# A gated cross-attention block: V products ahead of the value products, small products moved to their bank, the context transposed in a later step

## What is computed

```python
def xattn(x, context):                  # x is layernormed before, and again inside
    q = (layernorm(x, gamma, beta) @ w_q)        # 16 heads of 64
    k, v = split(context @ w_kv)
    attn = softmax(einsum('bqhd,bkhd->bhqk', q * SCALE, k))
    out = einsum('bhqk,bkhd->bqhd', attn, v) @ w_out + b_out
    return out * tanh(gate)
x = x + tanh(g_xattn) * xattn(layernorm(x), ctx)
x = x + tanh(g_ffn) * ffn(layernorm(x))
```

## Time and profile before

| | |
|---|---|
| median of three runs | 475.88 us (473.37 to 476.15) |
| span of the profiled execution | 473.7 us; the page gives no other time for it |
| PE busy | 439.7 us, 93% of the span |
| ACT busy | 386.4 us, 82% |
| DVE busy | 360.3 us, 76% |
| POOL busy | 356.6 us, 75% |
| instructions | 13155 |

### The profile page before, as it was taken

The page is one execution under the profiler, slowest core; times in us unless marked ns, Lnnn a source line. Parts: engine busy times, 40 slices in busy tenths (PEclk is TensorE's granted clock), DMA queues, the critical chain, the costliest instruction groups (busy, mean ns, idle before and its releaser), DMA issues.

```text
span 473.7 us, 13155 instructions
## 1 busy us (share of the span) xinstructions
PE 439.7 (93%) x5096; PEld 334.0 (71%) x5096; DVE 360.3 (76%) x789; ACT 386.4 (82%) x630; POOL 356.6 (75%) x270
## 2 busy tenths in 40 slices
PE   7889799998999989999999999999999999988993
PEld 6656667776767767776777667776777677758892
DVE  4787687778877887779787796878877887785622
ACT  5889788899888988899888898899799998892330
POOL 3687686888788887888878877898878877871325
PEclk9999999999999999999999999999999999999998
DMA  5499999999999999999999999999989998996021
GB/s 167 150 177 192 206 187 175 170 181 204 188 176 188 210 194 180 192 192 192 198 189 197 189 196 191 185 200 209 190 157 185 193 180 147 159 182 137 14 67 46
DMA packets 283037, 82.10 MB, mean 173 GB/s; under 512 B 264387, under 2 KB 280435, under 8 KB 282976
## 3 DMA queue, kind: packets, MB, share of 16 engines
q1 hardware_dynamic: 281600, 77.96, 93.4%
q0 software_dynamic: 1376, 3.30, 2.2%
HBM read 10.83 MB, written 5.14 MB: 34 GB/s over the span
## 4 chain that ended last, share of the span: by engine, by line
PE 40%; DVE 20%; ACT 16%; DMA 10%; issue 8%; POOL 4%; POOLq 0%; SPq 0%; ACTq 0%; DVEq 0%
DVE MXL L903 9%; DMA PT<-PARTS 9%; ACT P L752 7%; DVE HL L890 4%; ACT HL L714 4%; PE psAB L1234 3%; PE psX L1319 3%; PE psAB L1241 3%; PE psO L1267 3%; ACT PARTS L762 3%; POOL PARTS L650 3%; PE psX L1355 3%; DVE VL L896 3%; PE psO L1269 3%; PE psO L1268 3%
## 5 line engine op out<-in xcount | busy, mean ns | idle before, releaser
L650 POOL TENSOR_TENSOR PARTS<-P,PARTS 128x1024 f16<-128x1024 f32 x125 | 267.4, 2145 | 63.5 <-ACT PARTS L762 61.8
L762 ACT ACTIVATE PARTS<-P 128x1024 f16<-128x1024 f32 x126 | 136.1, 1080 | 0.7
L752 ACT ACTIVATE P<-psAB,NB 128x512 f32<-128x512 f32 x128 | 81.6, 695 | 41.8 <-DVE NB L906 41.4
L903 DVE TENSOR_REDUCE MXL<-psAB 128x2 f32<-128x1024 f32 x64 | 78.4, 1224 | 41.4 <-PE psAB L1241 23.9
L1267 PE MATMUL psO<-VH,PT 128*128 128x65 f16 x1008 | 98.6, 194 | 8.3 <-DMA PT<-PARTS 7.7
L1267 PEld LDWEIGHTS psO<-VH,PT 128*128 128x128 f16 x1008 | 92.0, 98 | 12.0 <-DMA PT<-PARTS 8.9
L1268 PE MATMUL psO<-VL,PT 128*128 128x64 f16 x1008 | 98.5, 192 | 0.0
L1269 PE MATMUL psO<-VH,PT 128*128 128x65 f16 x1008 | 98.4, 193 | 0.0
L1268 PEld LDWEIGHTS psO<-VL,PT 128*128 128x128 f16 x1008 | 91.3, 98 | 0.5
L1269 PEld LDWEIGHTS psO<-VH,PT 128*128 128x128 f16 x1008 | 91.5, 97 | 0.0
L752 ACT ACTIVATE P<-psCD,NB 128x512 f32<-128x512 f32 x128 | 81.7, 703 | 0.1
(11 more groups left out here) (214 smaller groups left out, 871.7 us busy)
## 6 DMA issues: line engine op xcount, KB each, us to landing
ctx_raw<-in_ctx_dram SPq DMA_DIRECT2D x8, 256.0 KB, 3.7
w1s<-in_L_ffn_w_dram SPq DMA_DIRECT2D x8, 256.0 KB, 3.6
w2s<-in_L_ffn_w_dram SPq DMA_DIRECT2D x8, 256.0 KB, 4.0
PT<-PARTS SPq DMA_TRANSPOSE x126, 5.0
experts_table<-zeros POOLq DMA_DIRECT2D x2, 645.0 KB, 4.0
X<-in_x_dram SPq DMA_DIRECT2D x8, 128.0 KB, 4.2
wraw<-in_L_xattn_w_kv_dram SPq DMA_DIRECT2D x4, 256.0 KB, 5.3
out_dram<-row SPq DMA_DIRECT2D x8, 128.0 KB, 2.5
```

Of the source, the lines that this page charges most:

```text
L650: pool.tensor_tensor(PARTS[:, par, qt, 1], P32[:, par, qt], PARTS[:, par, qt, 0], ALU.subtract).then_inc(plo_done, 1)
L752: last = act.activation(P32[:, par, qt, SK * h:SK * h + SK], score_bank(qt)[:, SK * h:SK * h + SK], ACT.Exp, bias=NB[:, par, qt, h:h + 1])
L762: act.activation(PARTS[:, hp % 2, qt, 0], P32[:, hp % 2, qt], ACT.Copy).then_inc(phi_done[qt], 1)
L903: dve.tensor_reduce(MXL[:, par, qt, :, 0], score_bank(qt)[:].rearrange("p (h n) -> p h n", h=2), AX.X, ALU.max, negate=True).then_inc(max_ ...
```

## The change

Four things are moved; no arithmetic is added or removed.

- The small products of all batches but the last write psO instead of psX. A second memory, `wait_o`, makes the next writer of psO wait for the last reader, and the value products go through it as well. psX keeps the V products and the context transposes (and the small products of the last batch behind the loop).
- On PE the small products and the context transposes stand right behind the scores, ahead of K and Q of the next pair. The V product of every step stands ahead of the value products.
- The context of the next batch is transposed in step 5 (`CTX_STEP` is 4 instead of 2, and the transposes stand one step behind it); ACT's and DVE's parts of it follow, and SP loads the next context in step 6 instead of 3.
- The readers: the copies of the transposed queries and tokens go from ACT to DVE, ahead of its second row maximum, as do the first reads of the expert choice and of the ranks. ACT's high part of V goes ahead of the second `phi`. `add_part` and `add_attention` stay where they were on DVE, behind `kq_lo`.

```diff
-        PART_STEP, CTX_STEP, PROJECT_STEP = 1, 2, 3
+        PART_STEP, CTX_STEP, PROJECT_STEP = 1, 4, 3
...
         def x_bank(b):
-            return psX[:, 0:SQ] if b else psO
+            return psO[:, 0:SQ]
...
# SP
-                    if hp == CTX_STEP + 1 and b + 2 < B:
+                    if hp == CTX_STEP + 2 and b + 2 < B:
                         sp.wait_ge(ctxt_psum, b + 2)
                         sp.dma_start(ctx_raw[:], ctx_t[b + 2]).then_inc(ctx_in, 16)
...
# ACT, batch
-                    if hp == X_STEP and not is_last(b):
-                        xt_copy(b + 1)
-                    if hp == TOKT_STEP and not is_first(b):
-                        tokt_copy(b - 1)
                     if j < LAST:
                         phi(b, hp, 0)
                     exps(b, hp, 1)
                     if ot_pair(j) >= 0:
                         ot_copy(ot_pair(j))
+                    if hp != CTX_STEP and v_group(b, hp):
+                        v_hi(*v_group(b, hp))
                     if j < LAST:
                         phi(b, hp, 1)
-                    if hp != CTX_STEP and v_group(b, hp):
-                        v_hi(*v_group(b, hp))
...
# DVE, new
+            def xt_copy(b):
+                dve.wait_ge(xt_psum, b + 1)
+                dve.wait_ge(norm_scaled, 1)
+                dve.wait_ge(xt_lo_done, b)
+                dve.tensor_scalar(XS[:], x_bank(b), norm_q[:, 0:1], norm_q[:, 1:2], ALU.mult, ALU.add)\
+                   .then_inc(xt_f32, 1)
+            def tokt_copy(b):
+                dve.wait_ge(tokt_psum, b + 1)
+                dve.tensor_copy(tT[:], psO[:, 0:QT * P]).then_inc(tokt_done, 1)
...
-            def add_part(b, part, bank=psX):
+            def add_part(b, part, bank=psO):
...
+            def take_ranks(b):
+                ranks = ps_ranks(b).rearrange("p (t e) -> p t e", e=E)
+                dve.wait_ge(pos_psum, b + 1)
+                dve.tensor_tensor(rank_hot[:], ranks[:, 0:QT, :], hot, ALU.mult).then_inc(route, 1)
+                dve.tensor_copy(taken[:], ranks[:, QT, :]).then_inc(route, 1)
...
# DVE, batch
-                    row_max(b, hp, 1)
+                    if hp == RANKS_STEP and b > 1:
+                        take_ranks(b - 2)
+                    if hp == X_STEP and not is_last(b):
+                        xt_copy(b + 1)
+                    if hp == TOKT_STEP and not is_first(b):
+                        tokt_copy(b - 1)
...
-                    if hp == LOGITS_STEP and not is_first(b) and not is_last(b):
+                    if hp == LOGITS_STEP and not is_first(b):
                         choose(b - 1)
+                    if j == LAST:
+                        take_ranks(B - 2)
+                    row_max(b, hp, 1)
+                    if hp == LOGITS_STEP and not is_first(b):
+                        first_winner(b - 1)
...
# PE
+            o_free = [None]
+            def wait_o(free_when):
+                if o_free[0]:
+                    pe.wait_ge(*o_free[0])
+                o_free[0] = free_when
...
             # values
-                if j:
-                    pe.wait_ge(norm_done, turn(j) - 1)
-                else:
+                wait_o((norm_done, turn(j)))
+                if j == 0:
                     pe.wait_ge(row_consts, 1)
...
-            def project_part(b, pairs, bank=psX):
-                if bank is psX:
+            def project_part(b, pairs, bank=psO):
+                if bank is psO:
+                    wait_o((part_done, b + 1))
+                elif bank is psX:
                     wait_x((part_done, b + 1))
...
             def project(b):
-                wait_x((x1_done, b + 1))
+                wait_o((x1_done, b + 1))
...
# PE, batch
                     scores(b, hp, 1)
+                    if hp == CTX_STEP + 1 and not is_last(b):
+                        ctx_transposes(b + 1)
+                    # ranks, project_part, project, x_transposes,
+                    # tok_transposes, router_weights, logits: here, as below
                     if ahead:
                         k_project(*next_pair(b, hp, AHEAD))
                         q_project(*next_pair(b, hp, AHEAD))
                     if ot_pair(j) >= 0:
                         o_transposes(ot_pair(j))
-                    # the same seven, and the V product of CTX_STEP among them
+                    if v_group(b, hp):
+                        v_project(*v_group(b, hp))
                     if VALUES_BEHIND <= j < LAST:
                         values(*back(b, hp, VALUES_BEHIND))
-                    if hp == CTX_STEP and not is_last(b):
-                        ctx_transposes(b + 1)
-                    if hp != CTX_STEP and v_group(b, hp):
-                        v_project(*v_group(b, hp))
```

More of the change, by code:

```diff
@@ L191, in gated_block, with ps_logits, ps_ranks @@
         psX = pb("psX", [P, 512])
-        ps_logits = psX[:, 0:QT * E]
-        ps_ranks = psX[:, 0:(QT + 1) * E]
-        ps_gw_mid = psX[:, 0:E]
+        def ps_logits(b):
+            return (psX if b == B - 1 else psO)[:, 0:QT * E]
+        def ps_ranks(b):
+            return (psX if b == B - 1 else psO)[:, 0:(QT + 1) * E]
+        ps_gw_mid = psO[:, 0:E]
         x_in = sem("x_in")
@@ L1018, in place @@
                 dve.tensor_copy(taken[:], ranks[:, QT, :]).then_inc(route, 1)
+            def place(b):
+                n = b * ROUTE
                 dve.wait_ge(lexp_done, b + 1)
@@ L1101, in _ @@
             normalise_heads(B - 1, PAIRS - 3)
-            add_part(B - 1, B - 1)
+            add_part(B - 1, B - 1, psX)
             normalise_heads(B - 1, PAIRS - 1)
@@ L1279, in o_transposes, with tok_transposes @@
                 last.then_inc(ot_psum, pairs)
-            def tok_transposes(b, bank=psX):
-                if bank is psX:
-                    wait_x((tokt_done, b + 1))
+            def tok_transposes(b, bank=psO):
+                if bank is psO:
+                    wait_o((tokt_done, b + 1))
                 pe.wait_ge(x1_done, B - 1 + QT if is_last(b) else b + 1)
@@ L1289, in logits @@
             def logits(b):
-                wait_x((route, b * ROUTE + 4))
+                (wait_x if b == B - 1 else wait_o)((route, b * ROUTE + 4))
                 pe.wait_ge(tokt_done, b + 1)
@@ L1293, in logits @@
                 for q in range(QT):
-                    last = pe.matmul(ps_logits[:, E * q:E * q + E], tT[:, P * q:P * q + P], gw_mid[:], start=True, stop=True)
+                    last = pe.matmul(ps_logits(b)[:, E * q:E * q + E], tT[:, P * q:P * q + P], gw_mid[:], start=True, stop=True)
                 last.then_inc(logit_psum, 1)
             def router_weights():
-                wait_x((gw_mid_done, 1))
+                wait_o((gw_mid_done, 1))
                 pe.wait_ge(gw_in, 16)
@@ L1332, in ranks @@
                 carried = taken[:].unsqueeze(1).to_broadcast([P, QT + 1, E])
-                pe.matmul(ps_ranks.rearrange("p (t e) -> p t e", e=E), ident[:], carried, start=True, stop=False)
+                pe.matmul(ps_ranks(b).rearrange("p (t e) -> p t e", e=E), ident[:], carried, start=True, stop=False)
                 for i, (counts, c) in enumerate(((tri, 2), (ones_bf, 1), (ones_bf, 0))):
-                    last = pe.matmul(ps_ranks, counts[:], hot_padded[:, c:c + QT + 1, :].rearrange("p t e -> p (t e)"),
+                    last = pe.matmul(ps_ranks(b), counts[:], hot_padded[:, c:c + QT + 1, :].rearrange("p t e -> p (t e)"),
                                      start=False, stop=(i == 2))
@@ L1349, in project @@
             def project(b):
-                wait_x((x1_done, b + 1))
+                wait_o((x1_done, b + 1))
                 pe.wait_ge(ot_done, b * PAIRS + PAIRS)
                 for qt in range(QT):
-                    dst = psX[:, D * qt:D * qt + D]
+                    dst = psO[:, D * qt:D * qt + D]
                     for pair in range(PAIRS // 2, PAIRS):
@@ L1386, in _ @@
             v_project(0, 0, 1, psO)
+            o_free[0] = (v_lo_done, 2)
             def batch(b):
@@ L1394, in batch @@
                     scores(b, hp, 1)
+                    if hp == CTX_STEP + 1 and not is_last(b):
+                        ctx_transposes(b + 1)
+                    if hp == RANKS_STEP and b > 1:
+                        ranks(b - 2)
+                    if j == LAST:
+                        ranks(b - 1)
+                    if hp == PART_STEP and not is_first(b):
+                        project_part(b - 1, range(PAIRS // 2))
+                    if hp == PROJECT_STEP and not is_first(b):
+                        project(b - 1)
+                    if hp == X_STEP and not is_last(b):
+                        x_transposes(b + 1)
+                    if hp == TOKT_STEP and not is_first(b):
+                        tok_transposes(b - 1)
+                    if hp == LOGITS_STEP and is_first(b):
+                        router_weights()
+                    if hp == LOGITS_STEP and not is_first(b):
+                        logits(b - 1)
```

39 lines of the change are left out of this document (9 added, 30 removed).

## The result

The changed kernel took 489.11 us (488.15 to 492.26, four runs), the kernel before on the same chip 475.98 (473.37 to 476.15). The ratio is 1.0317, 95% interval 1.0269 to 1.0364: 3.2% slower. The forecast was 498.4 with a range of 486 to 506. The profiled span grew from 473.7 to 486.9 us, so by 13.2 where the sum had 22.5.

The account below looks back on a forecast made before the run. The prediction took the tensor engine, 93% busy, as the bound. Its terms, 24.9 - 4.4 - 4.3 + 2.1 + 3.4 + 0.8 = 22.5 us, took the span from 473.7 to 496.2; with 2.2 more, 498.4 us, range 486 to 506.

Parts of the forecast that it names:

- the sum: Whole kernel: all predicted losses and gains together lengthen the profiled span of 473.7 us by 22.5 us.
- The holds: Steps 1 and 3, batches 1 to 7: value products wait for VectorE's additions, 14 times 1.78, 24.9 us.
- The context transposes: End of step 2: their wait behind the V product in psX goes, 0.73 in six batches, 4.4 us back.
- Waits of the scores: Second scores wait about 0.3 more in step 3 and 0.49 in step 5; 2.1 and 3.4 us in seven batches.
- Relief of the waits for PT: Value products wait less for transposed exponentials, four of six waits in steps 6 and 7: 4.3 us, ends 2.0 and 7.7.
- The last step: Its second row maximum starts later, behind the counts of ranks and two small reads: 0.8 us lost.
- what was open in the kernel before: Tensor engine, steady batch: matmuls fill 50.48 of 51.56 us, so little more than a microsecond is open to better order.
- The rule that was weighed: Tensor engine: by weight-load busy time, 14.15 us a batch are free; the prediction sided instead with closed-up matmul groups.
- the holds vanish in slack: Rival, steps 1 and 3: tensor engine slack absorbs the holds, only gains remain, 467.2 us; chance 0.05.
- no hold came in part only: Rival: split or addition comes sooner than batch 7 shows, say half of each hold, 486 us; chance 0.12.
- the transposes did not come late: Rival: context load pushes step 6's transposes by 1.15 in six batches, value products' waits not relieved, 509.6 us; chance 0.09.
- V ahead does nothing for these waits: Rival: the later fp16 copy eats the relief of the waits for transposed exponentials, 502.7 us; chance 0.1.

Follow-up runs that it names:

- experiment 1: Changed kernel with the two additions that read the half projections moved ahead of VectorE's split of the next K and Q; 471.5 us, ratio 0.9899.
- experiment 2: Changed kernel with the two half projections back behind the output transposes, still writing psO; 470.49 us, ratio 0.9886.
- experiment 5: Changed kernel with `CTX_STEP` set back from 4 to 2, so the next context is transposed in step 3; 490.52 us, ratio 1.0304.
- experiment 6: On top of experiment 1, token moments moved behind step 4's second row maximum, POOL's part a step later; 469.9 us, ratio 0.9914.
- experiment 4: On top of experiment 3, eight filler products into psX ahead of the value products in steps 1 and 3; 503.81 us, ratio 1.0611.
- experiment 3: Changed kernel with V product behind value products and ScalarE's V copy behind the second fp16 copy again, except step 4; 518.29 us, ratio 1.0861.

## Why the prediction was right, and which step of it was off

The sign, the place and the mechanism were right, and the time lay inside the range, 9.3 below the forecast (489.11 against 498.4). That the time fell inside the range is in part luck: the lower end was set for holds of half the length, and they came whole; the room was taken by gains that the sum had left out. By its own steps:

- **The holds.** Said: 14 times 1.78 in steps 1 and 3, 24.9 us. Measured: the time from the V product's start to the value products is 2.59 in steps 1 and 3 and 0.81 in the others, so 1.78 more, 14 times. Experiments 1 and 2 take the holds away, by moving the reader and by moving the writer, and the loss goes with them. They were priced from the kernel before, by the chain in batch 7, though nothing waited for that chain there.
- **The context transposes.** Said 0.73 a batch. From the start of the value products of step 2 to the next group it was 2.28 and is 1.55. Right; experiment 5 shows that the step number has no part in it.
- **Waits of the scores.** Said 0.3 in step 3 and 0.49 in step 5. Measured 0.34 (0.80 to 1.14) and 0.44 (1.20 to 1.64) in batches 1 to 6. For step 5 it had named the V copy and the moments; without that copy in step 4 (experiment 5) the wait is 0.50 shorter, with the moments later (experiment 6 against 1) 0.27, so both have a part. In batch 7 step 3 the second scores had waited more before (1.63, now 1.15), which the sum did not see.
- **Relief of the waits for PT.** Said 4.3 between 2.0 and 7.7, measured 6.8 (7.7 to 0.9): 2.5 better, inside its ends, but not where it was placed. The prediction looked for it in steps 6 and 7, behind grown steps; 4.1 of the 6.8 came in batch 0, which has no holds (4.3 to 0.2). For batches 1 to 7 (3.4 to 0.7) the runs do not agree: without the holds the waits there are 6.3 in experiment 1 and 1.0 in experiment 2. How much of the relief is due to V ahead, to the holds or to chance is open.
- **The last step.** Said 0.8. From the first scores of the last step to the end of the span the kernel took 0.6 more.
- **The step that failed: what was open in the kernel before.** The prediction ("What bounds the kernel now", "What the change takes away") counted only waits that the tensor engine's matmul rows show, and concluded that little more than a microsecond per batch was open. The weight loads of the small products had waits of their own for VectorE's split of V, and once a batch for that of the context, in the kernel before:

```profile
PEld psX L1294 <- DVE VL L896: 2.4, 7, 1.3
...
PEld psX L1319 <- DVE VL L896: 2.0, 7, 0.3
PEld psX L1365 <- DVE VL L896: 1.8, 7, 0.3
PEld psX L1286 <- DVE VL L896: 1.6, 7, 0.2
...
PEld psX L1355 <- DVE cT_lo L877: 1.1, 6, 0.2
```

These are 8.9 us of idle weight loads. But for 1.1 us (line 1294, once) no matmul row shows idle time there, since the rows ahead are drawn to overlap it. The starts show it: in steps 1 and 3 to 6 of the kernel before, the next group follows the output transposes by 0.33 to 0.42, where without a wait it follows by 0.16 to 0.22, depending on which group it is. Against 0.22 that is some 0.8 a batch. For the two projections experiment 2, which holds their place fixed, shows that it goes with the bank psX (0.20 and 0.11). For the other small products, which were moved in the order as well, it is argued from the same wait.

The account of the 9.3 us that the sum was too high on the span: 2.5 from PT. From the output transposes to the next group, and in the small products, the eight steps took 1.02 less per batch net, in batches 1 to 6 6.1, and 0.1 in batch 7; in that stands a new wait of 0.58 in step 4 (the V product there now waits for the split of V, seen above), without which it would be 1.6. The score waits of batch 7 came out 1.0 lower than the sum had them. In step 0 the scores took 0.14 more per batch, which gives back some 0.9. That makes 8.8 of 9.3; the rest is not placed. Part of the 1.02 is no wait but the account itself: a group's time to the next start depends on which group follows it. And the 2.5 from PT is little more than the 2 us by which these waits differ in batch 0 alone between two executions of the same instructions.

**The rule that was weighed.** The prediction set the closed sequence of matmul groups against the Trainium skill, Perfetto Trace Analysis, section Identifying the Most-Contended Engine, by which matmul busy time says little of how near TensorE is to its limit. For the holds the trace sided with the sequence: 1.78 came out as 1.78. For the gains it sided with the Trainium skill. The same 5096 matmuls were busy 439.7 us before and 435.1 after, in a kernel that waits more: what looked like a full engine held 8.9 us in which weight loads waited for a bank. The rival that the holds vanish in slack did not come about; the slack was there, elsewhere in the step.

The other rivals: no hold came in part only, and the transposes did not come late (0.9 us of waits for PT). That V ahead does nothing for these waits is not refuted: in experiment 4, where V stands behind the value products and the holds are there, they are 1.6.

## What to carry to other kernels

When a small product moves to another bank, look at where its reader stands on the reader's own engine. The bank's next writer then waits for everything queued ahead of that reader, here a split that itself depends on products issued later; the length of that chain can be read from the kernel before, even where nobody waits for it. To see how much a busy tensor engine has left, list the waits of its weight loads as well and compare start-to-start times of one group across steps, with the same group behind it: the differences show waits that overlapping matmul rows hide. And before a difference in waits between two profiles is put down to a change, look at a stretch that the change does not touch.

## What the runs showed of the hardware

In experiment 3 the lower granted clock came at 11 of 14 idle stretches of 2.35 us and slowed what stood behind it (values in up to 2.6 us instead of 1.45). In the changed kernel it came at none of the 14 holds with 1.65 us of idle time; the rows behind the holds keep 1.00:

```profile
288.00:291.00 3.00, 1.35 (x14) 1.00 1.31 163
291.00:300.00 9.00, 8.83 (x128) 1.00 1.05 212
```

The length of the idle stretch alone does not decide it. In the same execution of the changed kernel, in batch 0, the clock fell once behind an idle stretch of 1.60:

```profile
26.10 0.96 PE L1274 MATMUL psCD<-HL 64*128 64x512 f32 x6 [1.60 <-ACT P L753]
```

```profile
27.50:30.90 3.40, 3.40 (x26) 0.50 1.13 213
```

The 0.7 us more of waiting in each hold of experiment 3 (9.8 us over 14) so cost 15.9 us more, in the 11 steps with the lower clock. Filling the idle time with eight small products brought the clock back and 14.5 us with it (518.29 to 503.81).
